# Eight wide matmuls a step, written to a bank that nobody reads, in the recurrence loop of a four-layer gated block

## What is computed

```python
def step(carry, embed_t):
    h0, c0 = carry
    e = jnp.tanh(f_proj + (h0 @ Wh)[:, None, :])
    scores = jnp.einsum('bna,a->bn', e, v)
    alpha = jax.nn.softmax(scores, axis=-1)
    attn = jnp.einsum('bn,bnf->bf', alpha, feats)
    x = jnp.concatenate([embed_t, attn], axis=1)
    h0n, c0n = _lstm_cell(x, h0, c0, W_ih0, W_hh0, b_ih0, b_hh0)
    h1, c1 = _lstm_cell(h0n, h0n, c0n, W_ih1, W_hh1, b_ih1, b_hh1)
    return ((h0n, c0n), h1)
(_, _), outs = jax.lax.scan(step, (h0, c0), jnp.swapaxes(embeddings, 0, 1))
```

## Time and profile before

| | us |
|---|---|
| median of three runs | 6467.26 |
| lowest and highest | 6466.71, 6469.55 |
| span of the profiled execution, first to last instruction | 6458.9 |
| between the span and the median | 8.4 |
| TensorE busy in the span | 5126.0 |
| VectorE busy | 3339.5 |
| ScalarE busy | 2309.9 |

### The profile page before, as it was taken

The page is one execution under the profiler, slowest core; times in us unless marked ns, Lnnn a source line. Parts: engine busy times, 40 slices in busy tenths (PEclk is TensorE's granted clock), DMA queues, the critical chain, the costliest instruction groups (busy, mean ns, idle before and its releaser), DMA issues.

```text
span 6458.9 us, 202333 instructions
## 1 busy us (share of the span) xinstructions
PE 5126.0 (79%) x78350; PEld 3256.7 (50%) x78350; DVE 3339.5 (52%) x10049; ACT 2309.9 (36%) x6267; POOL 814.1 (13%) x1627
## 2 busy tenths in 40 slices
PE   7777777777777777777788889878898979888985
PEld 4666666666666666666433334433343233333443
DVE  3444444444444444444555553267767864555434
ACT  4333333333333333333334334321117944343432
POOL 1000000000000000000212220032210021222000
PEclk8555555555555555555789989989999979899997
DMA  1000000000000000000010000010000010000000
GB/s 56 0 0 0 0 0 0 0 0 0 0 0 0 0 0 0 0 0 0 39 46 39 19 26 0 0 63 33 32 7 1 0 79 20 39 39 7 2 1 13
DMA packets 17536, 90.71 MB, mean 14 GB/s; under 512 B 2344, under 2 KB 4648, under 8 KB 8872
## 3 DMA queue, kind: packets, MB, share of 16 engines
q1 hardware_dynamic: 17472, 89.88, 3.6%
HBM read 87.58 MB, written 2.29 MB: 14 GB/s over the span
## 4 chain that ended last, share of the span: by engine, by line
PE 59%; DVE 21%; ACT 10%; issue 9%; DMA 0%; DVEq 0%; SPq 0%; ACTq 0%
PE bank L924 14%; PE bank L935 12%; PE bank L447 9%; PE bank L485 6%; PE bank L462 4%; DVE arg L552 3%; ACT e L531 3%; PE bank L1406 3%; DVE xT L1032 3%; ACT ex L533 2%; DVE al L565 2%; DVE negmax L557 2%; ACT tc L541 2%; ACT t_ig L538 2%; DVE hp L590 1%
## 5 line engine op out<-in xcount | busy, mean ns | idle before, releaser
L1009 DVE TENSOR_TENSOR big<-sq,big 128x512 f16<-128x512 f32 x640 | 532.9, 834 | 729.8 <-ACT sq L994 725.4
L447 PE MATMUL bank<-al,wbuf 128*128 128x4 f16 x24576 | 737.6, 166 | 164.4 <-DVE al L565 164.4
L447 PE MATMUL bank<-hp,wbuf 128*128 128x4 f16 x24576 | 808.2, 166 | 0.0
L447 PEld LDWEIGHTS bank<-al,wbuf 128*128 128x128 f16 x24576 | 695.2, 104 | 206.9 <-DVE al L565 206.9
L447 PEld LDWEIGHTS bank<-hp,wbuf 128*128 128x128 f16 x24576 | 734.1, 104 | 86.0 <-issue 86.0
L994 ACT ACTIVATE big<-bank,vec 128x512 f16<-128x512 f32 x512 | 352.0, 687 | 906.3 <-PE bank L924 662.7
L924 PE MATMUL bank<-nT,hist_h 128*128 (+1 forms) x2304 | 573.3, 391 | 65.9 <-DVE big L1004 38.9
L531 ACT ACTIVATE e<-arg 128x256 f32<-128x256 f32 x1024 | 383.3, 417 | 635.8 <-DVE arg L552 635.8
L462 PE MATMUL bank<-hp,wbuf 128*128 128x4 f16 x6144 | 278.3, 169 | 412.0 <-DVE hp L590 409.4
L924 PE MATMUL bank<-nT,hist_s 128*128 (+1 forms) x2304 | 563.2, 386 | 35.2 <-DVE big L1004 35.2
L935 PE MATMUL bank<-big,hist_h 128*128 128x512 f16 x1920 | 483.7, 389 | 90.4 <-DVE big L1009 90.4
(11 more groups left out here) (357 smaller groups left out, 6608.4 us busy)
## 6 DMA issues: line engine op xcount, KB each, us to landing
wbuf<-in_f_w SPq DMA_DIRECT2D x32, 1024.0 KB, 8.3
big<-gates_of_layer SPq DMA_DIRECT2D x24, 1024.0 KB, 4.8
wbuf<-in_f_w SPq DMA_DIRECT2D x24, 512.0 KB, 6.6
xT<-in_xT SPq DMA_DIRECT2D x1, 2048.0 KB, 8.5
out_x<-big SPq DMA_DIRECT2D x16, 128.0 KB, 1.7
big<-in_x_w SPq DMA_DIRECT2D x1, 1536.0 KB, 6.5
hist_h<-in_w_at SPq DMA_DIRECT2D x1, 1024.0 KB, 10.7
nT<-in_w_x SPq DMA_DIRECT2D x1, 1024.0 KB, 12.7
```

The lines of the kernel that those rows point to most:

```text
L447: i = nc.tensor.matmul(GATE_OUT[g], w[:, part, k, g * P:(g + 1) * P], moving[:, k, lo * B:(lo + 1) * B], start=False, stop=False, skip_gro ...
L1009: nc.vector.tensor_tensor(lo, h, hi, ALU.subtract).then_inc(XL["hid"].sem, 1)
```

## The change

A helper `keep_busy(n, width)` issues n matmuls with the f16 identity as the weights and the first `width` columns of `whh` as the moving operand, into bank 7. It is called three times a step: twice 256 columns behind the forget gates' state part, twice 512 behind the other gates' state part, and four times 512 at the end of the step. Nothing reads bank 7 in the loop, and no semaphore is counted.

```diff
+        FILL_END, FILL_TANH, FILL_AL = ((4, 512), (2, 256), (2, 512))
+
+        def keep_busy(n, width):
+
+            for _ in range(n):
+                nc.tensor.matmul(bank[7][:, 0:width], ident16[:, :], whh[:, 0, 0, 0:width], start=True, stop=True)
+
...
                 state_part(GROUPS["f"])
+                keep_busy(*FILL_TANH)
 
                 for a in range(K):
                     pe.wait_ge(*R["act"].after(f"tanh{a}", t))
...
                 state_part(GROUPS["ig"])
                 state_part(GROUPS["o"])
+                keep_busy(*FILL_AL)
 
                 fig = ("f", "ig")
                 pe.wait_ge(*R["dve"].after("al_hi", t))
...
                         i = gate_mm(g, gat, al, j, ((0, 0), (1, 0), (0, 1)))
                 i.then_inc(R["pe"].sem, 1)
+                keep_busy(*FILL_END)
```

## The result

The changed kernel takes 7004.3 us (7004.03 to 7004.72 in four runs), the kernel before 6468.4 (6466.71 to 6469.55 in four runs beside them): a ratio of 1.0828, 95% interval 1.0815 to 1.0842, slower by 536 us. The spans of the two profiled executions are 7002.3 and 6458.9, 543.4 apart. The 8.4 us that the table of the kernel before gives between the span and the median do not lie around the span: each execution whose span is on record beside its time is 1.8 to 1.9 us longer than the span (7004.15 against 7002.3 here, 6461.16 against 6459.4 for the kernel before beside e1). So the profiled execution of the kernel before took, as an estimate, 6458.9 + 1.8 = 6460.7 us and was some 8 us quicker than the four timed ones; that is the difference between 543 and 536.

What follows compares the result with a forecast made beforehand. The recurrence, 46% of the span, was taken as a chain at TensorE's low clock with no engine full. Overruns 0.39 + 0.77 less 0.06 and 0.04 gave 1.06 us a step, 543 us: 7010, less 15, 6995; range 6180 to 7040.

Steps and rivals of the forecast that it cites:

- A: Forecast case: loop clock stays at 1.2 GHz but for stray pieces; 6995 us, range 6955 to 7050, chance 0.50.
- Which clock: TensorE's clock in the loop: taken to mostly stay at 1.2 GHz, with real doubt, since it doesn't follow the busy record.
- thin: Wide matmuls at 2.4 GHz would fill only 1.51 us of a 5.4 us step, less than stretches seen at full clock.
- rival B: Loop clock rises to 2.4 GHz within the first steps and holds; 6257 us, from 6165 to 6411, chance 0.39.
- AL: Two 512-column matmuls ahead of al's matmuls: 0.85 us against a 0.46 gap at 1.2 GHz, 0.39 late.
- the slow first load: Two runs of small matmuls lose their slow first load behind wide ones: 0.02 us each given back, 0.04 a step.
- TANH: Two 256-column matmuls ahead of the scores: 0.43 us against a 0.50 gap at 1.2 GHz, hidden.
- END: Four 512-column matmuls ahead of the next query: 1.71 us against a 0.94 gap at 1.2 GHz, 0.77 late.
- stray pieces: Pieces of the loop at the high clock, each saving up to 1.5 us of a step: 15 us taken off A.
- I take 16: Small f16 matmuls at 2.4 GHz taken as 16 ns instead of 27: 0.30 us a step saved ahead of t_f.
- the hand-offs: Lower end of rival B: a fifth of each of the chain's three 0.20 us hand-offs goes with the clock, another -0.12.
- Rival C: Clock alternates in the loop; break-even when 0.72 of steps are high, half and half gives 6636 us; chance 0.11.

Runs made afterwards that it cites:

- e1: Changed kernel with only END's four 512-column matmuls, without TANH and AL: 6809.69 us, ratio 1.0544 to the kernel before.
- e2: Changed kernel with fill cut to END 2 x 512, TANH 2 x 256, AL 1 x 512: 6459.75 us, ratio 1.0002 to the kernel before.
- e4: Changed kernel plus 48 matmuls of 128x512 once ahead of the loop: 7014.22 us, ratio 1.086 to the kernel before.
- e3: Changed kernel with TANH 3 x 512 and AL 3 x 512, END left at 4 x 512: 6827.91 us, ratio 1.0582 to the kernel before.
- e6: Changed kernel with END 5, TANH 4 and AL 3 matmuls of 512: 6542.33 us, ratio 1.012 to the kernel before.
- e9: As e6, but three of TANH's eight half-width matmuls moved between the two scoring passes: 6967.49 us, ratio 1.0776 to the kernel before.
- e5: Changed kernel without END, with TANH 2 x 256 and AL 2 x 512 kept: 6654.24 us, ratio 1.0294 to the kernel before.
- e7: As e6, but AL back at 2 x 512: 6871.34 us, ratio 1.0626 to the kernel before.
- e10: As e9, but two half-width matmuls between the scoring passes instead of three: 6932.39 us, ratio 1.0722 to the kernel before.
- e8: Changed kernel with TANH 7 x 256, one 256 ahead of the o gates' state part, AL 2 x 512, END 4 x 512: 6919.61 us, ratio 1.0701.

## Why the prediction was right, point by point

**The range.** 6180 to 7040 spans both levels of the clock, which had chances of 0.50 and 0.39, so a time inside it says little. What the result bears out is A: its own range, 6955 to 7050, the clock of the loop and the overruns of the step.

**Which clock.** Right in the outcome. The loop is at 0.50 from its second step on, and the loop of before was there throughout. The argument was that a record of "busy" isn't what the clock follows, and e2 and the changed kernel show that at its sharpest: 1600 of 1600 us busy, 0.50. One step of the argument failed: "The loop therefore starts at 1.2 GHz". The changed kernel enters it at 1.00 (the row of 112 to 114) and loses that in its first step, and so does e4. The outcome didn't depend on it. That the wide work is "thin" fits the order of the runs, in that e3 and e6, with more of it, were granted more, but it isn't the whole rule: e9 has e6's columns and doesn't hold the clock. What the clock follows stays open.

On this the Trainium skill's rule ("TensorE: Matmul & The Clock Gate", closing table), that keeping TensorE busy without a break gets the high clock, is what rival B stood on. Read by the busy time of a profile, it disagrees with the rows of the changed kernel and of e2: no idle time in the loop, and no high clock.

**AL, 0.39 forecast, 0.37 with the slow first load taken off.** The step shows 0.38, and e5 0.37 (190.7 / 512, TANH's part being nothing).

**END, 0.77 forecast, with 0.06 given back at the query.** 0.72 and 0.04 by the step, 0.687 net by e1. The forecast's 0.04 for two slow first loads was right in sum and not in place: behind each run of wide matmuls the next one starts 0.05 sooner than reckoned (2.02 after t_f where 0.36 + 1.71 makes 2.07; 2006.12 where 2005.32 + 0.85 makes 2006.17), and 0.03 is lost again between al's first matmul and t_f.

**TANH, nothing forecast.** Right: arg to negmax is 1.77 us before and after.

**The sum, 1.06 us a step, 543 us.** Right, by the spans to the microsecond; by the medians it is 536. That the hundredths of the terms cancel so well is in part luck. The 15 us taken off for stray pieces at the high clock had no ground: from 116 us on no piece of the loop shows one. With them the forecast came out 9 us low, without them it would have been 6 high.

**Rival B's price, 6257 with ends 6165 and 6411: mis-sized, in its own range.** B took 0.41 us a step off; the estimate from e3 and e4 is 5.84 - 5.64 = 0.20, so B would have ended at 6467 - 102 = 6365. The failed term is "that ratio makes 14 ns of the 27 ... I take 16" for the small f16 matmuls. A run of 36 takes (1.12 - 0.166) / 35 = 27 ns each at 1.2 GHz and (1.05 - 0.166) / 35 = 25 ns at 2.4 (e6). The router's f32 matmuls of the earlier trace rows were the wrong neighbour: their runs took 3.27 and 1.73 us at the two clocks, and these 1.12 and 1.05. So from negmax to t_f only 0.05 was gained (2.24 to 2.19) and not 0.30. The scoring gained about what was forecast: 0.12 from arg to negmax against 0.11. The hand-off from the gates to t_f gained next to nothing: in e6 t_f starts 0.87 us after the first of the matmuls that take al (2004.42 to 2005.29), and the 28th starts 27 x 0.025 = 0.68 after it, which leaves 0.19 where the low clock had 0.20. That speaks against the lower end of B, which let the hand-offs shrink; the other two were not measured by themselves.

The page that the prediction set against its 16 ns agrees here: the Trainium skill, "TensorE: Matmul & The Clock Gate", section on the 56 ns, has about 25 ns between the starts of small matmuls, and e6 shows 25. The 6380 that the prediction set beside its own figure is near the 6365 above.

**Rival C.** It wasn't what happened to this change, but it is what happened to five of the six denser mixtures (e3, e7 to e10), and its price was too low. The forecast mixed high and low steps by their share, so that it breaks even when 0.72 of the steps are high. In e9 half of the steps are wholly high and the others are at 0.77 in the mean, and it loses 0.98 us a step. A part of that is the denser fill itself, whose high step is 6.22. The rest is where the low stretch falls. In the step from 2011.02 to 2018.45 it falls on the five wide matmuls of END: each takes 0.43 us instead of 0.21, and arg (2013.93) comes 2.91 us after t_f instead of 1.83. That is 1.08 of the 1.21 between the two kinds of step.

**No version beats the kernel before.** The best with a fill is e2, which costs nothing and brings nothing. With the clock held, the loop has 0.20 us a step to win, and the mixture that held it (e6) overran by 0.32. Single steps were quicker than before, 5.75 us in e3 and e8, but not the loops around them. Whether some other placement holds the clock with less overrun isn't settled; e7 to e10 were four attempts, and all of them lost the clock.

## What to carry to other kernels

Ahead of raising a clock, ask what on the critical path would get faster by it: here it was 0.20 us of 5.84, because the small matmuls and the hand-off that was measured hardly follow TensorE's clock. Filler in an in-order queue is free only while it ends ahead of the next instruction's operands at the clock that is in fact granted; count it at the low clock first, and add up the overruns gap by gap, since they add. And read the granted clock itself, never the busy share, to see whether the filler did its work.

## What the runs showed of the hardware that was not expected

A loop can show TensorE busy in 100% of the time and be granted 1.2 GHz (the changed kernel from its second step on, e2). The same small f16 matmuls with four columns start 27 ns apart at 1.2 GHz and 25 ns apart at 2.4. The clock can alternate through the whole loop (mean 0.77 to 0.88 in e3 and e7 to e10), in e9 with every other step wholly high and the next one partly low, and kernels in that regime were slower than the same loop with no fill by 5.8 to 7.8%, slower even than e5, whose loop ran at the low clock and lost 2.9%. Moving three half-width matmuls from ahead of the scoring to between its passes, with the same number of columns in a step, took the loop's clock from 0.99 (e6) to 0.88 (e9).
